# A decoder's second layer: GpSimd adds the cross-attention's result, and its statistics come behind the next tile's self-attention

## What is computed

```python
x = x + _L1_attn_ref(_layernorm(x, axis=-1), L1_attn_Wq, ..., L1_attn_lam)
x = x + _L1_xattn_ref(_layernorm(x, axis=-1), ctx_2048, ctx_2048)
x = x + _L1_ffn_ref(_layernorm(x, axis=-1), L1_ffn_router_w, ...)
```

## Time and profile before

| what | value |
|---|---|
| three runs | 859.38, 856.19 and 860.75 us, median 859.38 |
| profiled execution, span from its first to its last instruction | 859.4 us (the page gives no other time for it) |
| mean granted TensorE clock | 0.956 of full speed |
| PE busy | 775.1 us, 90% of the span |
| DVE busy | 554.2 us, 64% |
| ACT busy | 384.4 us, 45% |
| POOL busy | 238.3 us, 28% |

### The profile page before, as it was taken

The page is one execution under the profiler, slowest core; times in us unless marked ns, Lnnn a source line. Parts: engine busy times, 40 slices in busy tenths (PEclk is TensorE's granted clock), DMA queues, the critical chain, the costliest instruction groups (busy, mean ns, idle before and its releaser), DMA issues. The chain is left out here.

```text
span 859.4 us, 15356 instructions
## 1 busy us (share of the span) xinstructions
PE 775.1 (90%) x5288; PEld 566.7 (66%) x5288; DVE 554.2 (64%) x1291; ACT 384.4 (45%) x847; POOL 238.3 (28%) x296
## 2 busy tenths in 40 slices
PE   6899878999999999997778999989989888999995
PEld 2455546878998999993335655555555537888884
DVE  3799946533432222223987999899996357888854
ACT  2466534332321111110334766666675407888860
POOL 2344420520000000004641433444431421434340
PEclk8999988999999999999899999899999798999999
DMA  9465441390289999836610001010125119999817
GB/s 337 176 245 223 189 153 56 94 405 16 78 296 387 388 345 316 304 137 158 203 34 2 25 11 45 25 51 31 46 82 208 56 42 347 411 396 393 336 56 251
DMA packets 57104, 158.03 MB, mean 184 GB/s; under 512 B 7180, under 2 KB 36748, under 8 KB 51708
## 3 DMA queue, kind: packets, MB, share of 16 engines
q1 hardware_dynamic: 51700, 141.97, 45.5%
q0 software_dynamic: 5328, 15.08, 4.9%
HBM read 114.21 MB, written 42.81 MB: 183 GB/s over the span
## 5 line engine op out<-in xcount | busy, mean ns | idle before, releaser
L1271 PEld LDWEIGHTS ps<-f_xT,f_rg 128*128 128x128 f32 x920 | 113.4, 192 | 5.2 <-DMA f_rg<-w_routed 1.7
L1271 PE MATMUL ps<-f_xT,f_rg 128*128 128x128 f32 x920 | 113.9, 275 | 1.3 <-DMA f_rg<-w_routed 1.3
L1176 DVE TENSOR_TENSOR f_rhT<-f_gate,ps 128x256 f32<-128x256 f32 (+1 forms) x69 | 25.9, 376 | 117.2 <-ACT f_gate L981 73.0
L2078 ACT ACTIVATE b_PX<-ps 128x512 f32<-128x512 f32 x128 | 72.7, 597 | 46.3 <-PE ps L2313 44.7
L1811 DVE TENSOR_REDUCE b_smax<-ps 128x4 f32<-128x1024 f32 x64 | 77.9, 1217 | 15.7 <-PE ps L2289 15.4
L981 ACT ACTIVATE f_gate<-ps 128x256 f32<-128x256 f32 (+1 forms) x69 | 24.0, 348 | 134.2 <-PE ps L1271 134.2
L2606 POOL DMA_INDIRECT y<-f_ys,f_to x47 | 45.1, 959 | 81.7 <-DVE f_to L2684 78.2
L1285 PE MATMUL ps<-f_rd,f_rhT 128*128 128x256 f32 x230 | 62.3, 387 | 0.0
L2313 PE MATMUL ps<-b_Q,b_Cx 100*128 100x256 f32 x256 | 55.8, 327 | 6.3 <-ACT b_PX L2078 6.0
L2313 PEld LDWEIGHTS ps<-b_Q,b_Cx 100*128 100x128 f32 x256 | 41.9, 206 | 26.6 <-ACT b_PX L2078 12.2
L1583 POOL MEMSET b_half<- 128x1 f32 x1 | 0.1, 99 | 212.9 <-POOLq L69 212.9
(11 more groups left out here) (333 smaller groups left out, 1843.1 us busy)
## 6 DMA issues: line engine op xcount, KB each, us to landing
f_rg<-w_routed SPq DMA_DIRECT2D x23, 1280.0 KB
rows<-a_blank SPq DMA_DIRECT2D x16, 1152.0 KB, 7.0
f_rd<-w_routed SPq DMA_DIRECT2D x23, 640.0 KB, 5.5
f_rw<-w_ffn SPq DMA_DIRECT2D x19, 704.0 KB
rw<-w_ffn SPq DMA_DIRECT2D x16, 704.0 KB
later<-w_ffn SPq DMA_DIRECT2D x12, 704.0 KB
f_xs<-rows SPq DMA_DIRECT2D x31, 144.0 KB
f_yk<-y SPq DMA_DIRECT2D x8, 512.0 KB, 7.8
```

The lines of the kernel that those rows point to most:

```text
L1271: mm = nc.tensor.matmul(ps[:, u % 4, k * P:(k + 1) * P], rg[b % R_SLOTS][:, off:off + P], xT[b % 2][:, c, :], start=(c == 0), stop=(c == C ...
L2078: nc.scalar.activation(PX[g % RING][:].rearrange("p c m -> p (c m)"), ps[:, RETS + G_TURN[g] % 2, :], ACT.Exp, scale=XSC).then_inc(turn_re ...
```

## The change

GpSimd gets a new function `add_crossed`, which waits for `crossed` and adds it to the rows of `X`; it is called ahead of `rsqrt(c_, 2)`. DVE's `add_cross` ends with the product in `crossed`. The statistics become a function of their own, `take_cross`, called behind `add_attention(a_)`, which waits for GpSimd's add. One semaphore is new. Nothing else differs.

```diff
+        cross_added = sem("cross_added")
...
+            def add_crossed(t):
+                if t is None:
+                    return
+                pool.wait_ge(read_cross, t + 1)
+                nc.gpsimd.tensor_tensor(X[:, t, :], crossed[:], X[:, t, :], ALU.add).then_inc(cross_added, 1)
+
...
                 if c_ == TILES - 1:
                     scatter(TILES - 2)
+                add_crossed(c_)
                 rsqrt(c_, 2)
                 rsqrt(a_, 1)
...
                 nc.vector.tensor_tensor(crossed[:], ps[:, OUT, 0:D], rden[:], ALU.mult).then_inc(read_cross, 1)
-                dve.wait_ge(read_cross, t + 1)
-                step.done(nc.vector.tensor_tensor(X[:, t, :], crossed[:], X[:, t, :], ALU.add))
-                step.wait()
+
+            def take_cross(t):
+                if t is None:
+                    return
+                dve.wait_ge(cross_added, t + 1)
                 normalise(X[:, t, :], 2, 2)
...
                 maxima(b_, 3)
                 add_cross(c_)
                 add_attention(a_)
+                take_cross(c_)
                 maxima(b_, 4)
```

## The result

The changed kernel takes 869.61 us in the median of six runs (862.57 to 873.62), the kernel before 858.80 us in six runs (856.19 to 860.75). The medians lie 10.8 us apart. The ratio on record, which isn't that of the medians, is 1.0133 with a 95% interval of 1.0103 to 1.0163, or 11.4 us (8.8 to 14.0). The forecast was 868 us, with a range of 861 to 875. In a second series of six runs on another occasion the ratio was 1.0136 (1.0088 to 1.0183), with medians of 867.15 against 857.34 us.

A forecast was written before the change was run, and what follows sets the result against it. The prediction took DVE to set the pace in five tiles, where work before a late projection was free. Terms of 6.0 (five full turns), 1.4 (sixth) and 1.0 (last two) gave 8.4 us on 859.4, about 868 us, range 861 to 875.

The forecast's parts named there:

- The bound: Five tiles running self-attention, two cross-attention stages and router together go at DVE's pace; DVE is busy 94.7% there.
- the faster rival: DVE sets the pace and has 0.46 us less work in eight tiles: 3.7 us faster, 855.7 us; chance 0.07.
- A full turn, +1.2 us: Each of five tiles with self-attention: c's statistics come later, delaying PE's turn of `row`; 1.2 us each, +6.0 us.
- DVE's idle time in front of the add: Sign: DVE idle 1 to 1.8 us before the self-attention's add, waiting for the projection, in five tiles and the sixth.
- PE's wait for `row`: Sign: PE's turn of `row` waits about 1.2 us for ACT in five tiles, about 2.2 in the sixth.
- a rival: PE makes up its 1.2 us stall at `row`, leaving DVE's 0.65 us per full turn: +4.4, 863.8 us; chance 0.15.
- The sixth turn, +1.4 us: Sixth tile, without new self-attention, where PE already waits for `row`: PE loses 1.4 us.
- The last two, +0.5 us each: Last two tiles, no self-attention to cover GpSimd's add of 0.85 us plus handovers: +0.5 us each, +1.0 together.
- The sum: 6.0 + 1.4 + 1.0 = 8.4 us on the span of 859.4, about 868 us.
- The clock: Rival: PE's new stalls in five tiles bring half-clock stretches, each costing 0.3 to 1 us; 873 us, chance 0.16.

The follow-up runs named there:

- the two filled kernels: Matmuls on idle data in PE's waits for `row`: changed kernel, first seven turns, 862.07 us; kernel before, sixth and seventh turns only, 856.13 us.
- the one experiment that takes the stall on `row` away: Changed kernel with PE's turn of `row` moved behind the next two first scores in PE's order; 868.09 us, ratio 1.0120.
- the two kinds of runs above: Changed kernel unaltered, twelve runs: five at mean granted clock 0.949 to 0.951 took 872.8 to 875.2 us, seven at 0.960 to 0.968 took 862.6 to 867.4.

## Why the prediction was right, point by point

**The bound.** Right. DVE sets the pace of the full turns, but its 94.7% were not all work that could be taken away: some of it stood where DVE would have waited. Taking work from DVE lowered its share to 88.3%, and the time rose by 1.3%. The rule of the Trainium skill (Perfetto Trace Analysis, Identifying the Most-Contended Engine), to optimize the engine with the highest occupancy first, would have given the faster rival if read as taking work from it; the trace disagrees with that reading.

**A full turn, +1.2 us.** Right. Undisturbed, the second turn is 31.44 us after and 30.29 before (with two later waits filled), +1.15; the first 31.77 and 30.60, +1.17. The third is 31.40 against 30.88, only +0.52, but the latter comes behind a turn with 6.8 us at half clock. The fourth and fifth of before are never undisturbed; between the two filled kernels the third to fifth differ by 0.95 to 1.06. DVE's idle time in front of the add was forecast at 1 to 1.8 us and is 1.14 to 1.75, PE's wait for `row` at 1.16 to 1.27 and is 1.21 to 1.22. What is open here is the price of a rival, that DVE's delay without PE's stall would cost only 0.65 us. DVE's own part is 0.72, but in the one experiment that takes the stall on `row` away 0.96 is left, for the late maxima and the later copy stall PE in turn. No run shows a turn in which the stall is absorbed.

**The sixth turn, +1.4 us.** Filled against filled, 25.37 - 23.92 = 1.45. Unfilled it is 27.66 - 25.51 = 2.15, with a mean clock of 0.88 where it was 0.93; I put the rest down to that, which is not shown. One sign was misread from the prediction's own sum: it gave PE's wait for `row` in this turn as about 2.2 us, which is what comes on top (645.16 - 642.99 = 2.17). With the 0.86 us of before the sum gives 3.03, and 3.06 was measured.

**The last two, +0.5 us each.** GpSimd's add takes 0.73 us, not 0.85. The wait for `row` grows from 2.45 to 2.79 and from 0.64 to 0.99, +0.34 and +0.35, a third less than the forecast's 0.5. As forecast, GpSimd's time mattered only where nothing covers it. The rule of the Trainium skill on the two engines (GPSIMD Engine Reference, Engine selection) gives about twice VectorE's time; the trace comes near it, with 0.73 against 0.42 us.

**The sum.** By these measured terms it is 5 x 1.15 + 1.45 + 0.34 + 0.35 = 7.9 us, where the forecast had 8.4. Turn for turn the two filled kernels differ by 1.25, 1.11, 0.95, 1.00, 1.06, 1.45 and 0.31 us, and the last wait by 0.34, 7.5 in all. Their ratios to the kernel before, 1.0048 and 0.9968, lie 0.8% or 6.9 us apart. The time of 868 us came out nearer than the sum, because it starts from 859.4 where the six runs have 858.80. That the span equals the median of three runs is chance: later runs take about 2 us more than the span of their execution.

**The clock.** The medians leave 2.9 of the measured 10.8 us (1.9 of 9.8 in the second series), the ratios 3.5 and 3.8. The mean granted clock accounts for a part at most. It is 0.958 over the twelve runs of the changed kernel and 0.961 over the 16 of the kernel before in the second series; the two kinds of runs above differ by 0.014 and by 7.9 us, so a difference of 0.003 would be worth some 1.6 us, as an estimate. The rest stays open.

What was mis-sized is the price of a half-clock stretch, which the rival took as 0.3 to 1 us from what DVE waited before. In the full turns of the kernel before these stretches come about 20 us behind `crossed`, and there one of 3.4 us costs 0.1 to 0.2 us (30.80 against 30.60; 31.85 against 31.77). Right behind the wait for `row`, one of 3.4 us cost 1.2 (32.60 - 31.44). The two turns with 6.8 us there, and 3.4 more some 24 us behind `crossed`, lost 3.0 and 2.8 (34.79 - 31.77 and 34.27 - 31.44). So the price depends on where in the turn the clock falls.

The rival's 873 us is what five of twelve runs took, against a chance of 0.16. Its mechanism is seen in the one of them that was profiled, but makes only about half of that execution's distance to the other profiled one; the rest lies ahead of the first `crossed`. That the rival's number came out so well is in part luck. The medians, 869.6 and 867.2, lie on both sides of 868.

## What to carry to other kernels

Before work is taken from the busiest engine, or moved behind another step, look at what stands next on that engine and when its input comes: work in front of a late input is free as long as it fits in there. Moved behind, it is on the critical path twice, once on its own engine and once for all that wait for its result. And where TensorE waits for 2 us and more in a dense stretch, look at the granted clock around it. Matmuls on idle data in a wait of 2.45 us shortened that turn by 4.1 us in one profile; over twelve runs, two filled waits gained 2.7 us (0.3 to 5.2).

## What the runs showed of the hardware that was not expected

The granted clock behind equal waits differs from one execution to the next. A wait of 1.22 us in PE's work was followed by 6.8 us at half clock in the first two turns of one execution, by none in the next three, and by none in the same two turns of another execution. In or right behind one of 2.4 to 3.1 us a stretch at half clock began in every profile that has it unfilled, ten times in six profiles. What such a stretch costs depends on its place: 3.4 us at half clock cost 0.1 to 0.2 us about 20 us behind `crossed`, and 1.2 us right behind the wait for `row`. The spread of the changed kernel's runs, 862.6 to 875.2 us, goes with the mean granted clock, 0.968 to 0.949, and that of the kernel before does likewise.
